# Queries and keys in two fp32r parts instead of three bf16 parts, two heads in 64-row tiles, and maxima and exponential units that alternate between the tiles

## The chip, the cores and the metric

One NeuronCore of a Trainium2 chip runs the whole program. The metric is device time in microseconds (us), from the first to the last instruction and what lies around them. The median of three runs of the kernel before is 1060.07 us (1059.28 to 1060.69).

## What is computed

The reference is a small transformer block on `x` of 4 x 1024 x 256 in float32: a mixture layer, a causal attention with 16 heads of 16, and the mixture layer again.

```python
def _L0_attn_ref(target, w_qkv, w_proj, b_proj, ln_gamma, ln_beta):
    qkv = target @ w_qkv                       # 256 -> 3 x 256; q, k, v: (4, 16 heads, 1024, 16)
    ...
    scores = einsum('bhqd,bhkd->bhqk', q, k) * (1.0 / np.sqrt(HD))      # HD = 16
    scores = scores * causal - (1.0 - causal) * NEG
    attn = softmax(scores, axis=-1)
    out = einsum('bhqk,bhkd->bhqd', attn, v)
    x = out @ w_proj + b_proj + target
    return (x - mu) * rsqrt(var + EPS) * ln_gamma + ln_beta

def _L0_ffn_ref(x, w_router, b_router, w_experts, b_experts):
    # router softmax over 8 experts, the best two chosen, their outputs added
    ...
x = x + 0.5 * ffn(layernorm(x))
x = x + attn(layernorm(x))
x = x + 0.5 * ffn(layernorm(x))
```

## The kernel before

**Stages.** The program has three stages that share the engines. The *front* (0 to about 340 us) runs the first mixture layer over eight chunks of 512 tokens (`NCH`), and for each finished chunk makes the values (`values`, L766) and the queries and keys (`queries_keys`, matmuls in `pair_product`, L346). The *attention* (about 340 to 823 us) runs over 16 groups (`NG`) of four heads of one batch element. The *back* (to the end) projects, normalises and runs the second mixture layer. Neighbouring stages overlap by a few steps: the front's last chunk already works on the maxima of group 0, and `lead` puts steps of the back between the blocks of the last two groups.

**Queries and keys.** A bank of 128 features x 512 tokens of float32 is split into three bf16 parts: ScalarE copies the first part out (`qk_hi`, L605), VectorE subtracts it (`qk_rests`, L992), ScalarE copies the second part (`qk_mid`, L609) and GpSimd subtracts that (`low_parts`, L469). SyncE stores the parts to `q_parts` and `k_parts` in HBM and `load` (L1256, L1258) brings them back for each group, into `qs` and `ks` with the 16 features of a head repeated in six pieces: 96 rows (`ROWS`), four heads side by side. The six pieces are the products of parts that are kept. Three more rows, 96 to 98, hold ones in `ks` and the negated maximum of each query, split in three bf16 parts, in `qs`.

**Attention, on each engine.** Each group needs two passes over the scores.
- *Maxima.* TensorE makes scores with queries on the partitions (`max_scores`, L1295, one of 38 `munits` per bank of 512 columns) and, for a block on the diagonal, adds the mask with one more matmul of 128 columns (L1298: `ident_b` times `masked_b`). VectorE reduces each bank to row maxima (`max_read`, L1322). After the last unit TensorE transposes the maxima (L1288), and VectorE splits them in three parts (L1307 to L1317), which SyncE places in the rows 96 to 98 of `qs` (L1347).
- *Exponentials.* TensorE makes the scores again with keys on the partitions and 99 rows, so that the maximum is subtracted (`exp_unit`, L1449, 38 units), ScalarE takes the exponential of each bank into `probs` (L1428), and GpSimd clears what lies above the diagonal (L1401).
- *Products.* For each of 12 blocks of keys, TensorE multiplies `probs` by the values (`products`, L1465) in float32, four heads at once in four tiles of 32 columns.

**Order.** It is written out by hand. In the slot of group g, TensorE issues an exponential unit of g, then one entry of a stream of maxima: the units from number 14 on of group g + 1, then three new ones of g + 2, the transpose for g + 1, and the rest of the first 14 of g + 2. The products stand a block or two behind their exponentials. Maxima have three banks (`ms`), exponentials three (`es`), outputs two (`os`). TensorE takes its instructions in order: a maximum unit waits until VectorE has read the bank three units back (`mread`), an exponential unit until ScalarE has read its bank (`expd`).

**In the last chunk of the front**, 16 maximum units of group 0 stand between the expert products (`takes_first`), 19 more between the steps behind it (`first_scores`, `FIRST`). The first of them waits for the constants of the mask, which GpSimd makes in `ready_group0`.

## Time and profile before

| | |
|---|---|
| median of 3 runs | 1060.07 us |
| the profiled execution, its own time | 1059.8 us |
| its span, first to last instruction | 1058.1 us |
| TensorE matmul busy | 1006.5 us, 95% |
| VectorE busy | 812.5 us, 77% |
| ScalarE busy | 533.6 us, 50% |
| GpSimd busy | 264.0 us, 25% |

A busy share is the union of an engine's instructions. The ends of matmuls are modelled, so matmuls that follow each other closely are seen best by the distance of their starts. The rows in the section below come from the page and from views of the trace: groups of instructions by shape, instructions in order of time, the waits, the chain of work that ended last, and busy time by stretches. In the chain a row is what held up the end at that time.

### The profile page before, as it was taken

Reading aid. Unit: us, or ns where it says so; the run is one execution under the profiler, and the core shown is the slowest. Engines: PE = TensorE matmul, PEld = TensorE weight load, DVE = VectorE, ACT = ScalarE, POOL = GpSimd, SP = SyncE. Lnnn points to the kernel's source line nnn. Section 1 sums busy time; section 2 is a strip of 40 time slices with the busy share of each in tenths; the row PEclk is TensorE's granted clock in tenths of the full one; section 3 lists DMA queues with packets and bytes.
Section 4 is the critical chain, followed back from the end, with each engine's and each line's share of the span. In section 5 each row is a group of like instructions: output and inputs, shape, how many; then the busy total and the mean of one; then the engine's idle time right before and its main releaser. Section 6 shows DMA issues by size and latency. Waiting matters only on the chain.

```text
span 1058.1 us, 20904 instructions
## 1 busy us (share of the span) xinstructions
PE 1006.5 (95%) x6050; PEld 606.7 (57%) x6050; DVE 812.5 (77%) x1795; ACT 533.6 (50%) x1042; POOL 264.0 (25%) x290
## 2 busy tenths in 40 slices
PE   6899999999987999999999999999987899999998
PEld 4677878787654343444444344433433677777776
DVE  5776767685766888888888888888857788888775
ACT  4225433543232677667777777777767423323210
POOL 1012211221323222221111111122322544344311
PEclk9999999999988899999999999999999999999999
DMA  7201101133144555544444555555130111101001
GB/s 231 65 1 61 60 0 59 60 81 42 57 89 91 62 72 73 66 60 62 59 62 62 62 71 71 72 72 73 35 103 9 51 61 61 50 28 42 20 21 40
DMA packets 55034, 63.99 MB, mean 60 GB/s; under 512 B 13776, under 2 KB 37312, under 8 KB 54976
## 3 DMA queue, kind: packets, MB, share of 16 engines
q1 hardware_dynamic: 54384, 62.47, 31.8%
q8 instruction: 29, 0.48, 0.2%
q10 hardware_dynamic: 592, 0.80, 0.2%
q14 instruction: 29, 0.24, 0.1%
HBM read 41.30 MB, written 21.23 MB: 59 GB/s over the span
## 4 chain that ended last, share of the span: by engine, by line
PE 86%; DVE 6%; ACT 3%; issue 2%; DMA 1%; POOL 1%; SPq 1%; DVEq 0%; POOLq 0%; ACTq 0%
PE bank L346 35%; PE bank L1465 14%; PE bank L1449 13%; PE bank L1295 13%; PE bank L766 3%; PE bank L1298 3%; PE bank L338 2%; PE bank L785 2%; ACT b_probs L1428 1%; DVE b_neg L1322 1%; DMA v_all<-L_ffn_w_experts 1%; DVE c_acc L982 1%; PE bank L735 1%; DVE a_st L301 0%; DVE a_acc L982 0%
## 5 line engine op out<-in xcount | busy, mean ns | idle before, releaser
L1322 DVE TENSOR_REDUCE b_neg<-bank 128x1 f32<-128x512 f32 (+3 forms) x608 | 366.0, 653 | 66.1 <-PE bank L1298 39.0
L1428 ACT ACTIVATE b_probs<-bank 128x512 f32<-128x512 f32 (+1 forms) x608 | 311.0, 577 | 132.6 <-PE bank L1449 130.8
L1295 PE MATMUL bank<-b_ks,b_qs 96*128 96x512 bf16 (+3 forms) x768 | 235.1, 336 | 16.1 <-DVE b_neg L1322 10.3
L1449 PE MATMUL bank<-b_qs,b_ks 99*128 99x512 bf16 (+3 forms) x768 | 222.2, 332 | 3.1 <-ACT b_probs L1428 2.7
L346 PE MATMUL bank<-we,a_xt 128*128 128x512 f32 x768 | 191.4, 402 | 1.9 <-DVE a_acc L982 1.9
L346 PE MATMUL bank<-we,c_xt 128*128 128x512 f32 x768 | 187.7, 399 | 1.9 <-DVE c_acc L982 1.9
L1401 POOL TENSOR_SCALAR_AFFINE_SELECT b_probs<-b_probs 128x512 f32<-128x512 f32 x128 | 83.0, 648 | 368.7 <-ACT b_probs L1428 368.6
L1465 PE MATMUL bank<-b_probs,b_vs 128*32 128x512 f32 (+3 forms) x1536 | 164.5, 500 | 1.7 <-POOL b_probs L1401 1.4
L346 PEld LDWEIGHTS bank<-we,a_xt 128*128 128x128 f32 x768 | 143.0, 191 | 31.7 <-DVE a_acc L982 1.6
L346 PEld LDWEIGHTS bank<-we,c_xt 128*128 128x128 f32 x768 | 141.8, 188 | 33.4 <-DVE c_acc L982 2.4
L1449 PEld LDWEIGHTS bank<-b_qs,b_ks 99*128 99x128 bf16 x768 | 65.8, 98 | 159.4 <-ACT b_probs L1428 119.0
L1295 PEld LDWEIGHTS bank<-b_ks,b_qs 96*128 96x128 bf16 x768 | 75.1, 99 | 65.7 <-DVE b_neg L1322 34.8
L1298 PE MATMUL bank<-b_masked_b,ident_b 128*128 128x128 bf16 x512 | 101.3, 223 | 0.0
L982 DVE SCALAR_TENSOR_TENSOR a_acc<-bank,a_mask,a_acc 128x256 f32<-128x256 f32 x192 | 81.5, 477 | 22.4 <-PE bank L346 21.4
L982 DVE SCALAR_TENSOR_TENSOR c_acc<-bank,c_mask,c_acc 128x256 f32<-128x256 f32 x192 | 81.5, 477 | 21.8 <-PE bank L346 21.3
L463 POOL TENSOR_TENSOR xs<-a_acc,a_acc 128x256 f32<-128x256 f32 (+1 forms) x32 | 24.8, 775 | 226.9 <-DVE a_acc L982 226.9
L1298 PEld LDWEIGHTS bank<-b_masked_b,ident_b 128*128 128x128 bf16 x512 | 51.1, 100 | 24.5 <-issue 0.3
L1465 PEld LDWEIGHTS bank<-b_probs,b_vs 128*32 128x32 f32 x1536 | 30.4, 108 | 55.8 <-issue 44.8
L463 POOL TENSOR_TENSOR xs<-c_acc,c_acc 128x256 f32<-128x256 f32 (+1 forms) x32 | 28.8, 900 | 99.9 <-DVE c_acc L982 99.9
L346 PE MATMUL bank<-a_xt2r,a_wqk 128*128 128x512 f32 x192 | 46.3, 396 | 0.8 <-DVE b_neg L1322 0.8
L469 POOL TENSOR_TENSOR a_part<-a_rest,a_part 128x512 bf16<-128x512 f32 x32 | 36.6, 1165 | 41.3 <-ACT a_part L609 41.3
L319 ACT ACTIVATE c_std<-c_mv,eps 128x4 f32<-128x4 f32 x16 | 4.6, 296 | 78.3 <-DVE c_mv L306 78.2
(134 smaller groups left out, 918.4 us busy)
## 6 DMA issues: line engine op xcount, KB each, us to landing
b_qs<-q_parts SPq DMA_DIRECT2D x96, 128.0 KB, 6.8
b_ks<-k_parts SPq DMA_DIRECT2D x96, 128.0 KB, 7.5
q_parts<-a_part SPq DMA_DIRECT2D x16, 384.0 KB, 2.7
k_parts<-a_part SPq DMA_DIRECT2D x16, 384.0 KB, 2.7
att_num<-b_oev SPq DMA_DIRECT2D x64, 64.0 KB, 7.6
c_num<-att_num SPq DMA_DIRECT2D x8, 512.0 KB
c_rec<-att_rec SPq DMA_DIRECT2D x16, 256.0 KB
out<-xs SPq DMA_DIRECT2D x8, 512.0 KB, 3.1
```

The costliest lines, as they stand in the source:

```text
L346: last = nc.tensor.matmul(out_, wa if x_moves else xa_, xa_ if x_moves else wa, start=(n == 0), stop=(n == len(steps) - 1))
L463: pool.tensor_tensor(s.xs[:, row(c, t), :].rearrange("p a d -> p (a d)"), acc[t % 2][0][:], acc[t % 2][1][:], ALU.add).then_inc(q.x_ready, 1)
L469: pool.tensor_tensor(part[j][:, 2, :], rest[j % 2][:], part[j][:, 1, :], ALU.subtract).then_inc(q.qk_lo, 1)
L766: last = nc.tensor.matmul(pt[pair][:, i * D:(i + 1) * D], xt2[:, h, t * P:(t + 1) * P], s.wv[:, h, :], start=(h == 0), stop=(h == DK - 1))
L982: dve.scalar_tensor_tensor(out=dst[:], in0=ring[n][:, i * D:(i + 1) * D], scalar=mask[par][:, t, 2 * n + i:2 * n + i + 1], in1=base, op0=A ...
L1295: last = nc.tensor.matmul(ms[bank][:, a * width:(a + 1) * width], qs[g.u][0:ROWS, c, i * P:(i + 1) * P], ks[g.u][0:ROWS, c, lo:lo + width] ...
L1298: last = nc.tensor.matmul(ms[bank][:, (a + 1) * width - P:(a + 1) * width], s.ident_b[:], masked_b[:], start=False, stop=True)
L1322: dve.tensor_reduce(dst, ms[bank][:, 0:len(heads) * width].rearrange("p (h w) -> p h w", w=width), AX.X, ALU.max, negate=True).then_inc(mr ...
L1401: pool.affine_select(out=part, in_=part, compare_op=ALU.is_ge, fill=0.0, base=0, pattern=[[0, GH], [1, P]], channel_multiplier=-1).then_in ...
L1428: act.activation(probs[b % 3][:, heads[0]:heads[0] + hp, 0:width], es[exp_bank(g, unit)][:, 0:hp * width].rearrange("p (h w) -> p h w", w= ...
L1449: last = nc.tensor.matmul(es[exp_bank(g, unit)][:, a * width:(a + 1) * width], ks[g.u][:, c, j * P:(j + 1) * P], qs[g.u][:, c, first_q:fir ...
L1465: last = nc.tensor.matmul(os_[half][SLOT * c:SLOT * (c + 1), start:CH], vs[g.u][:, j, c, :], probs[b % 3][:, c, 0:width], start=(j == 0), ...
```

## The change

- **Parts.** Queries and keys are split in two fp32r parts: ScalarE copies the first (`qk_hi`), VectorE subtracts (`qk_rests`) straight into the second. `qk_mid` on ScalarE and `low_parts` on GpSimd are gone. The parts in HBM are two of float32 instead of three of bf16.
- **Rows.** A head has three pieces of 16 rows, 48 rows (`ROWS`), and two rows for the maximum, 50 (`MROWS`). Two heads stand above each other: rows 0 to 49 and rows 64 to 113, and two pairs side by side. So a score matmul now names a tile of 64 rows x 128 columns, number t = 0 or 1.
- **Units.** Each unit of maxima or exponentials lies in one tile, and consecutive units of either kind change the tile. Group g still has 38 units of maxima; the exponentials have 40, since blocks of 128 columns hold two heads instead of four per unit. The stream of maxima keeps its order, but the transpose no longer takes a place when the stream is laid against the exponential units.
- **Mask.** It has 64 rows too and is added by two bf16 matmuls, of 128 and 64 columns, instead of one of 128. Its constants `pick` and `masked` take two memsets and four affine selects on GpSimd instead of one of each.
- **Maxima.** VectorE makes their two parts with two instructions instead of five; SyncE places them with four transfers instead of three.
- **Ones.** The rows of ones in `ks` come by two small transfers per buffer from `s.ones` instead of three memsets on GpSimd.

```diff
-ROWS = 6 * HD
-MROWS = ROWS + 3
-PARTS = ((0, 3), (3, 2), (5, 1))
+ROWS = 3 * HD
+MROWS = ROWS + 2
+PAIR = GH // 2
+HALF = P // 2
+Q_PARTS, K_PARTS = (0, 0, 1), (0, 1, 0)
...
-        def low_parts(m):
-            for j in range(4):
-                pool.wait_ge(q.qk_mid, at(4 * m + j + 1))
-                pool.tensor_tensor(part[j][:, 2, :], rest[j % 2][:], part[j][:, 1, :],
-                                   ALU.subtract).then_inc(q.qk_lo, 1)
...
-        def qk_mid(m, j):
-            act.wait_ge(q.qk_rest, at(4 * m + j + 1))
-            act.activation(part[j][:, 1, :], rest[j % 2][:], ACT.Copy).then_inc(q.qk_mid, 1)
...
                 dve.wait_ge(q.qk_hi, at(4 * m + j + 1))
-                dve.wait_ge(q.qk_lo, at(4 * m + j - 1))
-                dve.tensor_tensor(rest[j % 2][:], ring[j][:], part[j][:, 0, :], ALU.subtract).then_inc(q.qk_rest, 1)
+                dve.tensor_tensor(part[j][:, 1, :], ring[j][:], part[j][:, 0, :].bitcast(F32),
+                                  ALU.subtract).then_inc(q.qk_rest, 1)
...
+    pairs = [[(0, 0, P, p) for p in range(PAIR)] + [(CH // P, CH, P, p) for p in range(PAIR)]]
+    for i in range(1, KT):
+        for lo in range(0, (i + 1) * P, CH):
+            width = min(CH, (i + 1) * P - lo)
+            if (i, lo) == (CH // P, CH):
+                continue
+            if 2 * width <= CH:
+                pairs.append([(i, lo, width, p) for p in range(PAIR)])
+            else:
+                pairs += [[(i, lo, width, p)] for p in range(PAIR)]
+    return [(t, pieces) for pieces in pairs for t in range(2)]
...
-    return [[range(c, c + CH // width) for c in range(0, GH, CH // width)] for _, _, _, width in key_blocks()]
+    return [[(t, range(p, p + hp)) for p in range(0, PAIR, hp) for t in range(2)]
+            for hp in (min(PAIR, CH // width) for _, _, _, width in key_blocks())]
...
-        qs[u], ks[u] = sb(f"qs{u}", [MROWS, GH, SEQ], BF16), sb(f"ks{u}", [MROWS, GH, SEQ], BF16)
+        qs[u], ks[u] = sb(f"qs{u}", [P, PAIR, SEQ], F32R), sb(f"ks{u}", [P, PAIR, SEQ], F32R)
...
+            last = nc.tensor.matmul(ms[bank][:, begin:end], qs[g.u][rows, p, i * P:(i + 1) * P],
+                                    ks[g.u][rows, p, lo:lo + width], start=True, stop=not diagonal)
             if diagonal:
-                last = nc.tensor.matmul(ms[bank][:, (a + 1) * width - P:(a + 1) * width], s.ident_b[:],
-                                        masked_b[:], start=False, stop=True)
+                nc.tensor.matmul(ms[bank][:, end - P:end], pick[half, HALF:3 * HALF], masked[half, :],
+                                 start=False, stop=False)
+                last = nc.tensor.matmul(ms[bank][:, end - HALF:end], pick[half, 0:2 * HALF], masked[half, 0:HALF],
+                                        start=False, stop=True)
...
-            t, r, m = turned, turned_rest, mparts[g.u]
-            dve.tensor_copy(t[:], ms[bank][0:GH * KT, 0:P]).then_inc(mread, 1)
...
+            dve.tensor_copy(m[:, 0, :], turned).then_inc(mpart, 1)
+            dve.wait_ge(mpart, at(g.n + 1))
+            dve.tensor_tensor(m[:, 1, :], turned, m[:, 0, :].bitcast(F32), ALU.subtract).then_inc(mread, 1)
...
-                    while entries and entries[0][0] < unit0[b] + n:
+                    while entries and entries[0][0] - (entries[0][0] > turn_at) < unit0[b] + n:
```

**On TensorE, in the loop of the attention**, at the end of a block of 512 columns. `b_qs`, `b_ks` are queries and keys of a group, `b_probs` the exponentials, `b_vs` the values. Before:

```order
L1446 REGISTER_ALU
L1449 MATMUL bank<-b_qs_49,b_ks_50 128x512
L1285 REGISTER_ALU
L1295 MATMUL bank<-b_ks_74,b_qs_73 128x384
L1298 MATMUL bank<-b_masked_b,ident_b 128x128
L1465 MATMUL bank<-b_probs_56,b_vs_53 32x512 x4
```

After:

```order
L1470 REGISTER_ALU
L1475 MATMUL bank<-b_qs_49,b_ks_50 128x512
L1298 REGISTER_ALU
L1313 MATMUL bank<-b_ks_72,b_qs_71 128x384
L1316 MATMUL bank<-b_masked,b_pick 128x128
L1318 MATMUL bank<-b_masked,b_pick 128x64
L1492 MATMUL bank<-b_probs_56,b_vs_53 32x512 x4
```

The order of exponential unit, maximum unit and products is the same; a diagonal maximum unit has one matmul more. Along the stream the tiles of the score units run 0, 1, 1, 0, 0, 1, 1, 0: an exponential unit and the maximum unit behind it are in different tiles.

**On GpSimd, in the front before its last chunk**, where the mask's constants are made. `a_part` are the parts of queries and keys, `a_acc` the mixture's sums. Before:

```order
L463 TENSOR_TENSOR xs<-a_acc_108,a_acc_109 128x256
L469 TENSOR_TENSOR a_part_117<-a_rest_121,a_part_117 128x512
L469 TENSOR_TENSOR a_part_118<-a_rest_122,a_part_118 128x512
L469 TENSOR_TENSOR a_part_119<-a_rest_121,a_part_119 128x512
L469 TENSOR_TENSOR a_part_120<-a_rest_122,a_part_120 128x512
L1274 MEMSET b_masked_b 128x128
L1277 AFFINE_SELECT b_masked_b<-b_masked_b 128x128
L1267 MEMSET b_vs_72 128x32x16
```

After:

```order
L468 TENSOR_TENSOR xs<-a_acc_104,a_acc_105 128x256
L1275 MEMSET b_masked 128x128
L1276 MEMSET b_pick 128x192
L1280 AFFINE_SELECT b_pick<-b_pick 128x64
L1283 AFFINE_SELECT b_masked<-b_masked 128x64
L1287 AFFINE_SELECT b_pick<-b_pick 64x64
L1290 AFFINE_SELECT b_masked<-b_masked 64x64
L1271 MEMSET b_vs_70 128x32x16
```

The four subtractions ahead of the constants are gone and four instructions have come to them.

## Rows read from the trace of the kernel before

**Rows 1.** Stretches: length, busy us of PE, PEld, DVE, ACT, POOL, clock, DMA, GB/s.

```profile
343.20:353.30 10.10, 9.12 (x31) 3.54 (x32) 8.83 (x17) 3.86 (x7) 4.11 (x2) 0.50 0.68 88
370.30:744.80 374.50, 372.76 (x2929) 152.12 (x2927) 316.49 (x584) 265.94 (x521) 73.56 (x117) 1.00 0.52 66
773.50:824.00 50.50, 41.65 (x262) 16.93 (x263) 30.78 (x81) 35.72 (x69) 15.60 (x17) 0.94 0.14 39
```

**Rows 2.** The transposes of the maxima, one per group, between 365 and 750 us.

```profile
L1288 PEld LDWEIGHTS bank<-ident,b_neg x14: 97/97/97, 370.3 to 744.8; 128*32 128x32 f32 x14
```

**Rows 3.** Waits between 400 and 700 us: us in total, times, longest.

```profile
DVE b_neg L1322 <- PE bank L1298: 23.2, 51, 0.7
DVE b_neg L1322 <- PE bank L1295: 17.0, 31, 0.6
PEld bank L1295 <- DVE b_neg L1322: 11.7, 35, 0.7
```

**Rows 4.** TensorE in order of time in the loop: start us, length us, engine, line.

```profile
505.87 0.38 PE L1295 MATMUL bank<-b_ks,b_qs 96*128 96x512 bf16 x1
506.18 1.07 PE L1465 MATMUL bank<-b_probs,b_vs 128*32 128x512 f32 x8
507.18 0.39 PE L1449 MATMUL bank<-b_qs,b_ks 99*128 99x512 bf16 x1
507.41 0.38 PE L1295 MATMUL bank<-b_ks,b_qs 96*128 96x512 bf16 x1
507.63 0.38 PE L1449 MATMUL bank<-b_qs,b_ks 99*128 99x512 bf16 x1
...
508.50 0.22 PE L1298 MATMUL bank<-b_masked_b,ident_b 128*128 128x128 bf16 x1
508.56 0.38 PE L1449 MATMUL bank<-b_qs,b_ks 99*128 99x512 bf16 x1
```

**Rows 5.** TensorE in the front: fp32r matmuls, with a bf16 one between them.

```profile
22.17 0.23 PE L728 MATMUL bank<-ident_b,a_mask 128*128 128x128 bf16 x1
22.21 1.64 PE L346 MATMUL bank<-we,a_xt 128*128 128x512 f32 x6
...
152.24 4.12 PE L346 MATMUL bank<-a_xt2r,a_wqk 128*128 128x512 f32 x17
```

**Rows 6.** VectorE's split of the maxima between 400 and 700 us: busy us, mean ns.

```profile
L1317 DVE TENSOR_TENSOR b_mparts<-b_turned_rest,b_mparts 32x128 bf16<-32x128 f32 x11 | 4.7, 425 | 1.8 <-DVE b_mparts L1315 1.1
L1313 DVE TENSOR_TENSOR b_turned_rest<-b_turned,b_mparts 32x128 f32<-32x128 f32 x11 | 3.1, 280 | 0.4
L1307 DVE COPY b_turned<-bank 32x128 f32<-32x128 f32 x10 | 2.7, 269 | 0.0
L1311 DVE CAST b_mparts<-b_turned 32x128 bf16<-32x128 f32 x11 | 2.4, 215 | 1.1
```

**Rows 7.** The last chunk of the front, TensorE and GpSimd in order of time.

```profile
259.20 0.74 POOL L463 TENSOR_TENSOR xs<-a_acc,a_acc 128x256 f32<-128x256 f32 x1 [8.68 <-DVE a_acc L982]
267.49 0.29 POOL L1277 TENSOR_SCALAR_AFFINE_SELECT b_masked_b<-b_masked_b 128x128 bf16<-128x128 bf16 x1
...
267.84 0.23 PE L1295 MATMUL bank<-b_ks,b_qs 96*128 96x128 bf16 x1 [2.51 <-POOL b_masked_b L1277]
268.50 2.91 PE L346 MATMUL bank<-we,a_xt 128*128 128x512 f32 x6
```

**Rows 8.** The chain that ended last, at the seam from front to attention.

```profile
304.49 2.29 POOL a_part L469 x2
...
341.06 0.19 DVE b_turned L1307
...
343.65 0.48 DVE b_neg L1322
```

**Rows 9.** The weight loads: those of the attention (bf16) and of the front (f32).

```profile
L1295 PEld LDWEIGHTS bank<-b_ks,b_qs 96*128 96x128 bf16 x500 | 48.3, 98 | 26.4 <-DVE b_neg L1322 11.7
L346 PEld LDWEIGHTS bank<-a_xt2r,a_wqk 128*128 128x128 f32 x144 | 27.0, 188 | 6.5
```

174 lines of the change are left out of this document (96 added, 78 removed).

## The prediction

> **What bounds the kernel now.** I read the stretches first. In the steady part of the attention TensorE is busy 372.8 of 374.5 us, VectorE 316.5 and ScalarE 265.9, at the full clock [rows 1]. Fourteen transposes, one per group, start from 370.3 to 744.8 us [rows 2], so a group takes 374.5 / 13 = 28.8 us, of which VectorE works 24.3 and ScalarE 20.5. A busy TensorE can be a modelled one, so I looked at the distances of its starts. In the loop an exponential and a maximum matmul of 512 columns follow each other after 0.22 us (507.41 to 507.63), which is 512 columns at 2.4 GHz, its upper level; a mask costs 0.06 us (508.50 to 508.56), and the products of 512 columns hold it from 506.18 to 507.18, 1.0 us, with 0.1 us in front of them (505.87 + 0.22 to 506.18) [rows 4]. The waits agree: VectorE waits for TensorE 40.2 us in 300, TensorE's weight loads for VectorE 11.7 us [rows 3]. TensorE is the bound, VectorE 4.5 us per group behind.
>
> TensorE's group, from these rows: maxima and exponentials are each 18,432 columns, 36 matmuls of 512, so 72 x 0.216 = 15.5 us; 32 masks x 0.057 = 1.8; the 12 products are 6 of 512, 2 each of 384, 256 and 128 columns, which by the 1.0 us for 512 and about 0.2 us less for each 128 come to 9.4 us, and their 12 entries to 1.2. Sum 27.9 us; the other 0.9 us is waiting and the loop's own cost.
>
> **The change: score matmuls in the steady loop.** The trace of before shows no two row tiles, so this price is bounded from both sides. Below: two neighbours in different tiles run at the same time and the pair costs one. The nearest row is the products': eight matmul records in 1.07 us, in four column tiles [rows 4]; float32 takes four passes of 512 columns, 0.85 us, so four heads pass in the time of one. Above: they don't overlap, and each costs what an fp32r matmul costs alone. That is (4.12 - 0.39) / 16 = 0.233 us by the run of 17 [rows 5], 8% more than the 0.216 of bf16. So 36 pairs cost between 8.4 and 16.8 us against 15.5 now. I take the overlap: the products show that this array runs tiles side by side when its order lets it, and the order here puts neighbours in different tiles (0, 1, 1, 0, ...), so each unit finds the other tile free.
>
> The masks spoil part of it. A weight load of fp32r takes 188 ns, one of the bf16 scores 98 [rows 9]. Between fp32r matmuls a bf16 one of 128 columns costs more than its columns: six fp32r matmuls behind one end 22.21 + 1.64 = 23.85, when without it they would need 5 x 0.233 + 0.39 = 1.56; with the 0.04 in front that is 0.12 us for it [rows 5], which I put down to the next weights not being loaded under something so short. The unit behind a diagonal maximum is in the same tile, and the unit behind that can't start earlier. So a pair with a diagonal maximum of one head costs about 0.23 + 0.06 + 0.12 = 0.41 us (0.35 at 384 columns), not 0.23. Of the 38 units 16 have no diagonal: 16 x 0.233 = 3.7 us. Sixteen have one: 16 x 0.38 = 6.1. Four have two of 256 columns, about 0.6 each: 2.4. Two have four of 128, about 1.1 each: 2.2. The two added exponential units: 0.2. Sum 14.6 us against 17.3, a gain of 2.7. The products stay at 10.6. TensorE then needs 25.2 us.
>
> The Trainium skill ("TensorEngine Tiling (Array Packing)", Tiling Modes) says that different tiles can execute weight loads and matmuls in parallel; an estimate by that page's rule alone would have the masks hidden as well and pairs and masks at about 9.5 us, the case of the first rival below. "TensorE: Matmul & The Clock Gate" (Weight-path perf modes) speaks against the change: the fast weight load is not for fp32. The trace agrees with the second (188 against 98 ns [rows 9]); no run here shows the first for row tiles.
>
> **VectorE in the loop.** The reductions are as many and as wide. The split of the maxima loses three of five instructions: 269 + 215 + 280 + 215 (L1315, as L1311) + 425 = 1.40 us and some 0.3 of waits between them become one cast and one subtraction, 0.6 us [rows 6]. VectorE falls from 24.3 to 23.3 us per group. ScalarE has two units more; at its 20.5 us for 38 units and two copies that is at most 1.0 us, and it stays under 21.6. So TensorE at 25.2 stays the latest, VectorE now only 1.9 behind it. With the 0.9 of waiting kept, a group takes 26.1 us; some of that waiting was the loop's own, and the masks' hidden share is unknown, so I take 25.8: 3.0 us less per group. From the first group's second half to the last but one that is 14 groups: **-42 us**.
>
> **Transfers.** A group's queries and keys were 12 transfers of 16 rows x 4 heads x 1024 x 2 bytes and are 12 of 16 x 2 x 1024 x 4, the same bytes in pieces twice as long; they lie behind other work. The four placements of the maxima start some eight units before they are needed. Cost nothing; if a group took under 23 us, the cover for loads and placements would be thin. The parts of queries and keys are stored as 512 KB instead of 384, also under other work.
>
> **The front.** ScalarE loses 32 copies, GpSimd 32 subtractions, but the front's TensorE sends fp32r matmuls at their own distance of 0.233 us [rows 5], so in chunks 1 to 7 this is worth nothing. In the last chunk it is: the first maximum unit waited 2.51 us for the mask's constants, which stood behind `low_parts`; the next six expert matmuls then took 2.91 us instead of 1.64 at the half clock (1.2 GHz) [rows 7, 5]. GpSimd is now free at 259.9 us and needs, at 0.35 us for each of six instructions, until 262, before TensorE asks at 265.3. That is -2.5 - 1.3 = -3.8 us. Against it, each of the 16 maximum units there now changes the tiling from 128 rows to 64 and back. The nearest row is 0.1 us for a change before the products [rows 4]; two of them, and 0.1 us for the narrow mask and the fp32r weights: 16 x 0.3 = +4.8. Sum +1.
>
> **The seam.** The chain goes through ScalarE's second copy and GpSimd's two subtractions, 304.49 + 2.29, before VectorE goes on with the last chunk; now one VectorE subtraction, 0.7 us, ends about 304.6: -2.3. Later the split of the first maxima, from 341.06 to 343.65 [rows 8], shrinks to 0.7: -1.9. Then 10 us at half clock (343.20 to 353.30) [rows 1] hold some 8 us of score matmuls, worth -3.5 when paired. Sum -7.7. **The last two groups**: from 773.5 to 824 ScalarE is busy 35.7 of 50.5 us and the work of the back lies between [rows 1]; -1 for both.
>
> **The sum.** -42 + 1 - 7.7 - 1 = -49.7 us on the execution of 1059.8, which is within 0.3 us of the median: **1010 us**, faster by 4.7%.
>
> **The rivals.**
> - *VectorE becomes the bound.* The tiles hide the masks too: 36 x 0.233 = 8.4 us for pairs and, with the masks halved, 1 us more. TensorE falls to about 20 us and the group to VectorE's 23.3 plus a little, say 24.1: 14 x 4.7 = -66, with the rest -8: about 986 us. For it: four column tiles overlap without a visible cost. Against it: the order of instructions, since the unit behind a mask is in its tile. 0.18.
> - *The overlap is partial*: it sets in only where both units are ready at once, and TensorE's waits for VectorE (11.7 us in 300 now) and ScalarE undo half of it. A group at 27.6: -17, and about 1036 us. 0.14.
> - *The tiles don't overlap for fp32r* (slower). Then the score matmuls cost 16.8 instead of 15.5, the masks 32 x 0.12 = 3.8 instead of 1.8 at most, 32 x 0.09 = 2.9 at least: +2.4 to +3.3, with two weight loads that don't fit under narrow matmuls up to +4. 14 x 3.2 = +45, the front +5, the seam -4: about 1105 us (1090 to 1125). It decides from the point where a pair of 512 columns takes more than 0.43 us from start to start. For it: no row shows two row tiles at once; 0.16.
> - *The clock falls in the loop*, because TensorE now waits for VectorE: before, it fell to half where TensorE had waited for single steps of VectorE (343.20, after the split of the maxima), and at half clock the pairs cost 0.43 as before while the products double to 2 us. Also slower, some 1150 us, but a TensorE at the half clock is again fully busy and would be granted more. 0.03.
> - *The change does little, since VectorE and ScalarE waited only for the products*: within 0.2%. 0.02.
>
> **How the numbers follow.** The forecast has 0.47 and its own range 998 to 1023: the group between 25.0 and 26.6 us. From VectorE's case at 984 to the partial case at 1050 it holds about 8 in 10; the cases without overlap are left out above. Faster by over 0.2% (about what a measurement of this kernel tells from no change): 0.47 + 0.18 + 0.14 = 0.79; within: 0.02; slower: 0.19.
>
> **What would show it.** In the loop two score matmuls of different tiles start within a few hundredths of a us of each other, and pairs 0.23 us apart without a mask, 0.4 with one. The distance of the transposes is 25.8 us. TensorE no longer waits for GpSimd near 265 us, and the first exponential unit of group 0 starts near 341 instead of 348. VectorE is over 88% busy in the steady part. I am wrong if the starts of score matmuls of both tiles lie 0.23 us apart, or if TensorE's weight loads wait for VectorE by over 2 us per group: then VectorE is the bound.

## The result and the profile after

The changed kernel takes **1114.45 us** (median of four runs, 1110.68 to 1119.98). The kernel before took 1060.01 us beside it (four runs, 1059.28 to 1060.69): the ratio is 1.0519, interval 1.0494 to 1.0544. The change is slower by 5.2%; the forecast was 1010 us, and 1114 lies outside its range. The profiled execution has a span of 1108.9 us against 1058.1.

The page gives the first hint. Its line of 40 slices for TensorE's granted clock reads, for the changed kernel:

```profile
PEclk9999999999787699978996997899998899999999
```

The stretches of the attention follow, with the columns of [rows 1]: first group, four groups, a stretch of 23 us, two groups.

```profile
353.60:385.00 31.40, 30.03 (x174) 16.70 (x172) 22.26 (x39) 14.56 (x27) 3.10 (x5) 0.57 0.38 54
387.90:473.80 85.90, 84.52 (x772) 46.51 (x771) 71.27 (x125) 61.38 (x126) 16.90 (x27) 1.00 0.44 68
484.00:507.00 23.00, 21.95 (x119) 11.01 (x121) 11.78 (x19) 11.27 (x22) 3.10 (x5) 0.50 0.56 77
513.50:570.90 57.40, 56.44 (x515) 31.02 (x514) 47.65 (x84) 40.92 (x84) 11.27 (x18) 1.00 0.43 68
```

There are two kinds of stretches. Where the clock is whole, a group still takes 28.6 us: the transposes lie as follows (as [rows 2]; 387.9 to 473.8 in three groups, then one group alone).

```profile
L1301 PEld LDWEIGHTS bank<-ident,b_neg x4: 94/94/94, 387.9 to 473.8; 128*32 128x32 f32 x4
...
L1301 PEld LDWEIGHTS bank<-ident,b_neg x2: 94/94/94, 473.8 to 513.5; 128*32 128x32 f32 x2
```

85.9 / 3 = 28.63 us, against 28.8 before: 0.2 us was won where 3.0 were forecast. And three groups of the loop, one in three, took 39.7, 39.1 and 39.9 us instead. In each of them TensorE ran at 1.2 GHz, half its clock, for 20 to 24 us, though it was busy nearly all the time (21.95 of 23.00 us above).

The 50.8 us of the span divide so: the first transpose comes at 353.6 instead of 339.9 (+13.7); the first group lasts 34.3 instead of 30.4 (+3.9); from the second transpose to the last, 387.9 to 819.2, it is 431.3 instead of 403.2 (+28.1: three long groups at +11.0 each, the rest a little under before); what follows, +5.1.

**The tiles do overlap.** TensorE in order of time, columns as [rows 4]:

```profile
548.20 0.38 PE L1475 MATMUL bank<-b_qs,b_ks 50*128 50x256 f32 x1
548.20 0.50 PE L1313 MATMUL bank<-b_ks,b_qs 48*128 48x512 f32 x1
...
551.90 0.50 PE L1475 MATMUL bank<-b_qs,b_ks 50*128 50x512 f32 x1
551.90 0.73 PE L1313 MATMUL bank<-b_ks,b_qs 48*128 48x512 f32 x2
552.24 0.40 PE L1475 MATMUL bank<-b_qs,b_ks 50*128 50x512 f32 x1
```

Two units in different tiles start within 10 ns, where before they stood 0.22 us apart. But the pair does not cost the 0.233 us of one of them here: the next pair starts 0.34 us later (551.90 to 552.24). That is so in all 17 places of the loop at the whole clock where a pair of 512 columns follows another; each time the first one stands directly behind products. Before, the two units took 0.44 to 0.45 us. The low price does exist, as a kernel of experiment 2 shows (the changed one without masks), where one pair stands behind products and the next one doesn't:

```profile
506.17 0.50 PE L1470 MATMUL bank<-b_qs,b_ks 50*128 50x512 f32 x1
506.17 0.73 PE L1313 MATMUL bank<-b_ks,b_qs 48*128 48x512 f32 x2
506.51 0.62 PE L1470 MATMUL bank<-b_qs,b_ks 50*128 50x512 f32 x2
506.74 0.39 PE L1313 MATMUL bank<-b_ks,b_qs 48*128 48x512 f32 x1
```

From 506.17 to 506.51 it is 0.34 us again, then 0.23 to 506.74. So the overlap is there, and still the group kept its length.

**A stop at one place of the loop.** The waits of TensorE between 387 and 745 us (as [rows 3]) hold a line that the kernel before has not:

```profile
PE bank L1475 <- issue: 9.0, 3, 3.0
```

Three times TensorE issues nothing for 3 us and nothing in the record holds it. In order of time, the first of them:

```profile
481.57 0.51 PE L1475 MATMUL bank<-b_qs,b_ks 50*128 50x128 f32 x3
485.05 0.91 PE L1475 MATMUL bank<-b_qs,b_ks 50*128 50x512 f32 x2 [2.97 <-issue]
```

The others follow 578.8 and 675.2 us; the granted clock falls near them, at 483.5, 582.4 and 678.0. Such a line is easily read past: it says "issue", nobody's wait, and 9 us in 358 is little. It holds the key, as experiment 6 shows.

### The profile page after: what moved, and what is told of

Same layout as the page of the kernel before. It is cut to its first block, busy times and chain, and to the rows that moved or that the text cites. A ratio compares the mean times of both kernels' runs of the same rounds, so it can differ in the third digit from the quotient of the medians.

```text
span 1108.9 us, 21845 instructions
## 1 busy us (share of the span) xinstructions
PE 1049.0 (95%) x6562; PEld 692.1 (62%) x6562; DVE 804.0 (73%) x1747; ACT 519.3 (47%) x1042; POOL 216.8 (20%) x260
## 3 DMA queue, kind: packets, MB, share of 16 engines
q1 hardware_dynamic: 44284, 66.90, 28.1%
## 4 chain that ended last, share of the span: by engine, by line
PE 85%; DVE 6%; ACT 4%; issue 3%; DMA 1%; SPq 0%; POOL 0%; DVEq 0%; ACTq 0%; POOLq 0%
PE bank L350 35%; PE bank L1475 15%; PE bank L1492 15%; PE bank L1313 9%; PE bank L756 3%; ACT b_probs L1452 3%; PE bank L1316 2%; PE bank L775 2%; PE bank L342 2%; DVE b_neg L1345 1%; PE bank L1318 1%; DMA v_all<-L_ffn_w_experts 1%; DVE a_st L305 1%; DVE c_acc L972 1%; PE bank L725 1%
## 5 line engine op out<-in xcount | busy, mean ns | idle before, releaser
L1452 ACT ACTIVATE b_probs<-bank 128x512 f32<-128x512 f32 (+2 forms) x640 | 313.7, 557 | 166.3 <-PE bank L1475 161.8
L1313 PE MATMUL bank<-b_ks,b_qs 48*128 48x512 f32 (+3 forms) x768 | 283.6, 451 | 10.2 <-DVE b_neg L1345 7.1
L1475 PE MATMUL bank<-b_qs,b_ks 50*128 50x512 f32 (+3 forms) x768 | 264.3, 435 | 19.5 <-ACT b_probs L1452 9.3
L1475 PEld LDWEIGHTS bank<-b_qs,b_ks 50*128 50x128 f32 x768 | 127.1, 203 | 176.0 <-ACT b_probs L1452 134.5
L350 PE MATMUL bank<-we,a_xt 128*128 128x512 f32 x768 | 195.9, 409 | 1.9 <-DVE a_acc L972 1.9
L1492 PE MATMUL bank<-b_probs,b_vs 128*32 128x512 f32 (+3 forms) x1536 | 179.4, 542 | 1.2 <-POOL b_probs L1425 1.1
L350 PEld LDWEIGHTS bank<-we,a_xt 128*128 128x128 f32 x768 | 145.1, 194 | 33.5 <-issue 1.8
L1313 PEld LDWEIGHTS bank<-b_ks,b_qs 48*128 48x128 f32 x768 | 141.1, 204 | 33.5 <-DVE b_neg L1345 17.8
L1316 PE MATMUL bank<-b_masked,b_pick 64*128 64x128 bf16 x512 | 112.3, 239 | 0.0
L972 DVE SCALAR_TENSOR_TENSOR a_acc<-bank,a_mask,a_acc 128x256 f32<-128x256 f32 x192 | 81.5, 478 | 30.4 <-PE bank L350 29.6
L1318 PE MATMUL bank<-b_masked,b_pick 64*128 64x64 bf16 x512 | 93.0, 197 | 0.0
L1316 PEld LDWEIGHTS bank<-b_masked,b_pick 64*128 64x128 bf16 x512 | 49.0, 100 | 21.1 <-issue 9.9
L1318 PEld LDWEIGHTS bank<-b_masked,b_pick 64*128 64x128 bf16 x512 | 50.5, 103 | 0.0
```

The source lines that it names most:

```text
L350: last = nc.tensor.matmul(out_, wa if x_moves else xa_, xa_ if x_moves else wa, start=(n == 0), stop=(n == len(steps) - 1))
L972: dve.scalar_tensor_tensor(out=dst[:], in0=ring[n][:, i * D:(i + 1) * D], scalar=mask[par][:, t, 2 * n + i:2 * n + i + 1], in1=base, op0=A ...
L1313: last = nc.tensor.matmul(ms[bank][:, begin:end], qs[g.u][rows, p, i * P:(i + 1) * P], ks[g.u][rows, p, lo:lo + width], start=True, stop=n ...
L1316: nc.tensor.matmul(ms[bank][:, end - P:end], pick[half, HALF:3 * HALF], masked[half, :], start=False, stop=False)
L1318: last = nc.tensor.matmul(ms[bank][:, end - HALF:end], pick[half, 0:2 * HALF], masked[half, 0:HALF], start=False, stop=True)
L1452: act.activation(probs[b % 3][:, lane:lane + hp, 0:width], es[exp_bank(g, unit)][:, 0:hp * width].rearrange("p (h w) -> p h w", w=width), ...
```

## The experiments

Times are of one run unless it is said otherwise, each beside the kernel before on the same chip (1056.2 to 1060.3). One caution on small differences: the front's fall of the clock near 270 us is absent in some profiled runs of the same front, lasts 6.8 us in others and 17.1 in others again, and the first transpose comes at 346.8 to 353.6 us accordingly. So I compare groups of the loop, not totals, where less than 10 us matters.

**1. Do half-array tiles lower the clock?** The kernel before with 48 rows in every score matmul, which puts them in a tile of 64 rows. The order and the other engines' programs stay (the exponential units are cut to 48 rows by the same edit, not shown below).

```diff
-                                    ks[g.u][0:ROWS, c, lo:lo + width], start=True, stop=not diagonal)
+                                    ks[g.u][0:48, c, lo:lo + width], start=True, stop=not diagonal)
...
-                last = nc.tensor.matmul(ms[bank][:, (a + 1) * width - P:(a + 1) * width], s.ident_b[:],
-                                        masked_b[:], start=False, stop=True)
+                last = nc.tensor.matmul(ms[bank][:, (a + 1) * width - P:(a + 1) * width], s.ident_b[0:64, :],
+                                        masked_b[0:64, :], start=False, stop=True)
```

> The kernel before, but both score passes multiply 48 of the 96 and 99 rows, and the mask 64 of 128, so that every score matmul lies in one tile of 64 rows (it leaves out half of the products of the scores and the subtraction of the maximum). The matmuls are as many, as wide and, in one tile, one behind the other; only the rows of the array in use change. Theory A (the granted clock falls because the array's rows are used less): the clock falls to half for stretches of the loop as in the changed kernel, mean clock 0.95 or below, and the time is 1080 to 1120 us. Rival B (it falls because TensorE waits more): TensorE waits no more than before, so clock 0.98 and 1060 us within 5.

1423.7 us. Two more sizes, the same edit with 64 and with 80 rows (80 need the tile of 128):

> As the run with 48 rows in one tile, but with 64 rows of the scores (two of six parts and the subtraction of the maximum left out), which fill the tile. If the number of rows in use within the tile sets the granted clock, 64 rows raise it well over the 0.70 of 48 rows. If it is the half array that stands idle, it stays near 0.70 and the time near 1420 us, and rows of zeros in the changed kernel's tiles would bring nothing.

> The same with 80 rows, which no longer fit a tile of 64, so that each score matmul lies in the tile of 128 rows (one of six parts and the subtraction of the maximum left out). Theory A in the form 'a matmul in a half tile counts for less': clock 0.98 and 1060 us, as the kernel before. If rows in use count in proportion: clock between, 0.8 to 0.95, 1100 to 1250 us.

The time with 48 rows is far above even what Theory A expected. 64 rows: 1420.0 us. 80 rows: 1056.1 us. The same stretch of the three kernels, 48 rows first, then 64, then 80:

```profile
400.00:700.00 300.00, 300.00 (x1279) 99.00 (x1277) 150.36 (x252) 129.19 (x228) 32.62 (x52) 0.50 0.30 38
```

```profile
400.00:700.00 300.00, 300.00 (x1275) 98.71 (x1275) 149.56 (x251) 128.45 (x227) 32.53 (x52) 0.50 0.30 38
```

```profile
400.00:700.00 300.00, 298.13 (x2363) 121.38 (x2359) 255.71 (x472) 213.32 (x418) 60.26 (x97) 1.00 0.53 67
```

TensorE is busy 300.00 of 300 us and has half its clock for all of them; a group takes 53.1 us. In fact the clock fell at 343.8 and stayed low for 798.7 us. With the rows in a tile of 128 it is whole. So it isn't the rows in use in proportion, since 48 and 64 do the same, but the tile (a limit in rows between 64 and 80 would look alike): in these kernels a single tile of 64 rows, one at a time, doesn't bring the clock back, though TensorE is never idle. The Trainium skill ("TensorE: Matmul & The Clock Gate", Part 1) has the clock follow how busy TensorE has been; by the busy share alone, 300 of 300 us, this clock would be whole, and the measurement decides.

**2. The masks.** Both kernels without the mask matmuls (causality is left out of the maxima, so they are not the reference's). In the changed kernel:

```diff
-                                    ks[g.u][rows, p, lo:lo + width], start=True, stop=not diagonal)
-            if diagonal:
-                nc.tensor.matmul(ms[bank][:, end - P:end], pick[half, HALF:3 * HALF], masked[half, :],
-                                 start=False, stop=False)
-                last = nc.tensor.matmul(ms[bank][:, end - HALF:end], pick[half, 0:2 * HALF], masked[half, 0:HALF],
-                                        start=False, stop=True)
+                                    ks[g.u][rows, p, lo:lo + width], start=True, stop=True)
```

> The kernel before without the mask matmuls of the maxima (the maxima are then taken over all keys of a block). At the full clock TensorE loses 32 x 0.06 = 1.8 us per group: if TensorE is the bound the transposes are 26.9 us apart instead of 28.7 and the time falls by about 27 us. If waits for VectorE and ScalarE hold the loop, under 1 us per group.

> The changed kernel without the mask matmuls of the maxima. If the masks between fp32r units in their tile are what ate the gain of the overlap (theory M), a group at the full clock falls from 28.7 to 25 us or less, twice and more what the kernel before gains by the same edit. If the loop waits for ScalarE and VectorE anyway (rival W), it stays above 27.

Before without masks: 1034.8 us, a group 27.1 (-1.7). After without masks: 1044.1 us, a group 26.4 (-2.3), between the 25 of theory M and the 27 of rival W, so neither alone; and the three long groups are gone. The changed kernel's transposes and a stretch:

```profile
L1301 PEld LDWEIGHTS bank<-ident,b_neg x12: 93/94/94, 432.9 to 722.8; 128*32 128x32 f32 x12
```

```profile
459.30:670.40 211.10, 204.87 (x1546) 94.87 (x1545) 187.95 (x337) 161.73 (x336) 45.22 (x72) 1.00 0.51 72
```

I read this as "masks in one tile let the clock fall". That was wrong, as 6 shows: with the masks, 384 instructions of TensorE leave the body of the loop too.

**3. The masks' order.** The masks of a unit in two matmuls behind all its scores:

```diff
+        if wide[0]:
+            k = len(pieces)
+            ends = ms[bank][:, 0:k * width].rearrange("q (a w) -> q a w", w=width)
+            nc.tensor.matmul(ends[:, :, width - P:width], pick[half, HALF:3 * HALF],
+                             masked[half, :].unsqueeze(1).broadcast_to([HALF, k, P]), start=False, stop=False)
```

> The changed kernel with the masks of a unit behind all its score matmuls, in two matmuls per unit instead of two per piece (the same columns): in six units of a group 16 pieces have 12 of each mask's weight loads and 10 changes from bf16 back to fp32r weights less. Theory M/A together (masks hold one tile alone, which costs time at the full clock and makes the half array stand idle): at 0.1 us each a group at the full clock falls by 1.0 us from 28.7 to about 27.7 and the clock falls less often; 1060 to 1085 us. If the masks of the other units decide, 1095 or more.

1110.9 us; a group at the whole clock 27.9 us (-0.8), the long ones 43.7, 43.2, 40.4. Then the tiles of the maxima exchanged, so that an exponential unit and the maximum behind it share a tile:

```diff
-    return [(t, pieces) for pieces in pairs for t in range(2)]
+    return [(t, pieces) for pieces in pairs for t in (1, 0)]
```

> The changed kernel with the two tiles of the maxima exchanged (1, 0 instead of 0, 1), so that a maximum unit stands in the tile of the exponential unit ahead of it and runs beside the one behind it. Theory M: now the masks run beside the next exponential unit; a pair with a diagonal costs about 0.32 instead of 0.41 us, so a group at the full clock takes 27.3 instead of 28.7 us and the time falls by 15 to 25 us. Rival W: 28.7 as before, since the waits are elsewhere.

1186.4 us; a group 30.3 (+1.7), and one half-clock stretch of 122.9 us. So the order of tiles is worth something, but the opposite one gains nothing. A strictly alternating one, the maximum unit ahead of every second exponential unit, alone and with the masks in two:

```diff
-                    exp_unit(g, b, n)
+                    if (unit0[b] + n) % 2:
+                        exp_unit(g, b, n)
...
+                    if (unit0[b] + n) % 2 == 0:
+                        exp_unit(g, b, n)
```

> The changed kernel with the maximum unit ahead of every second exponential unit, so that the tiles of the score units alternate strictly (0, 1, 0, 1) and never stand in pairs (0, 1, 1, 0). If the masks' chain in one tile stops the other tile because the next unit in order is in the same one (the working of the prediction), a diagonal pair goes from 0.41 to 0.32 us: a group at the full clock falls by up to 1.4 us, to 27.3 or more. If waits for ScalarE and VectorE decide, it stays at 28.7 or grows, as exchanging the tiles did (30.3).

> Both edits together: the masks of a unit in two matmuls behind its scores, and strictly alternating tiles. If they add, 26.5 to 27.3 us per group at the full clock, and the half array idles less, so that the clock holds in the loop as in the run without masks: 1050 to 1070 us. If the clock falls again in three places: 1095 or more.

1123.9 and 1106.5 us; groups of 28.8 and 27.9, no better than the kernels without it. And the bank of the transposed maxima given free by a copy, before they are split:

```diff
+            dve.tensor_copy(turned[:], ms[bank][0:GH * KT, 0:P]).then_inc(mread, 1)
```

> The changed kernel, with the transposed maxima copied to SBUF first and their bank released after that, as the kernel before has it (three instructions instead of two). In the trace of the changed kernel the gap between products around the transpose is 2.81 us against 2.00 before. If the late release causes it, it falls by about 0.3 us (one instruction of 280 ns on VectorE), and a group from 28.7 to 28.4; if it is VectorE's own work that counts, the third instruction makes it 0.2 us longer. The clock as in the changed kernel: 1105 to 1120 us.

1112.4 us, groups of 28.7 to 29.2: nothing gained.

**4. The front.** The kernel before with the mask's constants ahead of GpSimd's subtractions, and the changed one with four maximum units instead of 16 in the front's last chunk:

```diff
+                if isinstance(c, int) and c == NCH - 2:
+                    a.ready_mask(pool)
```

```diff
-FIRST = (16, 23, 34, 35)
+FIRST = (4, 23, 34, 35)
```

> The kernel before with one edit: GpSimd makes the constants of the mask ahead of the four subtractions of the query and key parts instead of behind them. If the price put on this part of the change is right (a wait of 2.5 us and 1.3 us at the half clock), 1056.2 us, faster by 0.3 to 0.4%. If something else is late there, or the subtractions are missed later, 1059 to 1061.

> The changed kernel with 4 instead of 16 maximum units between the expert products of the front's last chunk; the other 12 come behind it. If these single units in a half tile let the clock fall there (17 us at half from 271.8), the fall goes or shortens and the first transpose comes earlier than 353.6 or no later than 356, though VectorE has 12 reductions of 0.65 us more behind the chunk (7.8 us). If the fall has another cause, it stays and the transpose is 5 to 8 us later.

The first: 1057.92 us (ten runs, 1056.27 to 1059.16) against 1058.89 (thirteen), ratio 0.9992, interval 0.9982 to 1.0001. Taking away the wait of 2.51 us [rows 7] is worth about 1 us, 2 at the most and perhaps nothing by the interval, and the trace says why. TensorE in order of time:

```profile
265.27 1.62 PE L346 MATMUL bank<-we,a_xt 128*128 128x512 f32 x6
269.09 0.28 PE L1299 MATMUL bank<-b_ks,b_qs 96*128 96x256 bf16 x1 [2.21 <-DVE b_neg L1326]
```

The next wait, for VectorE's reductions of the four banks that TensorE has filled in a burst, is 2.21 us long. The second: 1114.9 us. The fall near 271 us is gone and the first transpose comes at 342.7 instead of 353.6. The edit is not shown to be the cause of that: the first of the alternating variants of experiment 3, with all 16 units in place, has no fall there either, and its first transpose comes at 346.8. The seam (305.4, 23.9 us long) and the turns (up to 37.5 us) hold longer half-clock stretches in this run, and the total is the same.

**5. Who holds the group at the whole clock?** The reductions of VectorE over half the columns (the maxima are then of half the keys), in the changed kernel, the one before, and the changed one without masks:

```diff
+        scores = scores[:, :, :, 0:width // 2] if len(pieces) > PAIR else scores[:, :, 0:width // 2]
```

> The changed kernel, with VectorE reducing only the first half of each head's columns in a bank (the maxima leave out half of the keys). TensorE, ScalarE and the order are the same; VectorE's reductions take about 0.26 us less each, 10 us per group. If VectorE's pace holds the group at 28.7 us at the full clock (rival W for VectorE), it falls by 2 us or more. If the masks' chain on TensorE and the waits for ScalarE hold it, it falls by under 1 us. The clock may fall oftener or less often; the distances at the full clock count, not the time.

> The same edit to the kernel before. TensorE is the bound there: the group stays within 0.3 us of 28.7, and the time within 10 us of 1060.

> The changed kernel without masks (26.4 us per group, VectorE 89% busy) and with half reductions. TensorE's own sum there is 8.4 for the pairs and 10.6 for the products, 19 us; ScalarE's is about 20.5. If VectorE held it at 26.4, it falls to 23 or less. If it is the turn-taking of ScalarE and TensorE over three banks and the products, it stays above 25.

1116.6, 1049.4 and 1019.0 us; groups of 27.8 (-0.8), 28.4 (-0.4, a little more than expected with TensorE as the bound) and 25.5 (-0.9 against the one without masks). In the last, none of the engines is near its bound but TensorE by its modelled busy time, and ScalarE and TensorE wait for each other. Its stretch, then its waits:

```profile
400.00:700.00 300.00, 291.18 (x2288) 132.86 (x2290) 174.04 (x494) 238.15 (x497) 66.98 (x107) 1.00 0.52 76
```

```profile
PEld bank L1471 <- ACT b_probs L1448: 121.9, 225, 0.8
...
ACT b_probs L1448 <- PE bank L1471: 60.3, 117, 1.0
```

Half of VectorE's work gives 0.8 us, all the masks 2.3, both 3.2, and then 25.5 us are left, when the overlapped score matmuls and the products come to 19.2 (36 x 0.233 + 0.2 + 10.6, by the prediction's terms). Where the other 6 us lie these runs don't separate. Some are the dearer pairs behind products, by my estimate up to 12 x 0.107 = 1.3 us (0.34 less 0.233 for each of the 12 products). For the rest the waits above point to the turns of ScalarE and TensorE: TensorE waits for ScalarE to read a bank, and ScalarE then for the next units, with products between them. No run changed the number of banks or moved the products, so this is my reading and not shown.

**6. What makes the clock fall in the loop.** First, more work in whole-array tiles: the products of the first block of keys issued twice.

```diff
+            for lane in (range(GH) if j == 0 else ()):
+                c = head(*divmod(lane, PAIR))
+                nc.tensor.matmul(os_[half][SLOT * c:SLOT * (c + 1), start:CH], vs[g.u][:, j, c, :],
+                                 probs[b % 3][:, lane, 0:width], start=True, stop=True)
```

> The changed kernel with each group's two products on key block 0 (512 columns, float32, all rows and all four column tiles) issued twice, the first result overwritten: 2 us more of work on the whole array per group, 32 us in all. Theory A (the clock falls where the whole array is used too little): the clock holds or falls in fewer places, so that the time is at most 1115 us in spite of the added work. If the clock doesn't depend on it: 1140 us or more.

1129.1 us, a group 30.4 (+1.75); the half-clock stretches of the loop last 27.3, 10.2 and 10.2 us instead of 23.9, 20.5 and 23.9. The time lies between the two expectations. The added whole-array work doesn't prevent the falls; whether it shortens them is open, since one stretch is longer and two are shorter, and other variants differ from each other as much. All three start at the same place of the loop. That sent me back to the "issue" line. TensorE's program loops over three groups. The body was 1337 instructions and is 1535 (matmuls and weight loads counted apart; the trace has 1630 and 1828 records in a turn, mostly since it shows each float32 matmul and weight load of the products twice); the queue that brings instructions moves, between 400 and 740 us, before and after (packets, MB, share):

```profile
q8 instruction: 5, 0.08, 0.1%
```

```profile
q8 instruction: 31, 0.51, 0.7%
```

The loop turns three times. Before, no packet of this queue comes between 455 and 725 us: the body is repeated without being fetched. Now it comes again each time. After the change there are 7 packets between 487 and 577 us, within one turn, and one between 481 and 484 us, where the first stop is:

```profile
q8 instruction: 1, 0.02, 2.0%
```

Every variant above fits: bodies of 1145 and 1151 (without masks) and 1337 never stop, those of 1415 (masks in two matmuls), 1535 and 1583 (products twice) stop at every turn, 2.8 to 3.5 us each. Two kernels separate the cause. One writes the loop out on TensorE alone:

```diff
-        slots(pe, slot)
+        for n in range(NG):
+            slot(Group(0, 0) + n)
```

> The changed kernel with TensorE's loop over the groups written out (the 12 slots of the attention's loop stand one after the other, no branch; the other engines keep their loops). The records show that TensorE issues nothing for 3.3 us at 481.7, 578.8 and 675.2 us, each time at the turn of the loop, one of 3 groups, whose body on TensorE has grown from 1337 to 1535 instructions; q8, the queue of instructions, moves 31 packets between 400 and 740 us, 5 in the kernel before. 1.8 to 3.6 us after each of these stops the granted clock falls. Theory A (half-array tiles alone let the clock fall): the three stops go, -10 us, and the clock falls anyway somewhere in the loop; the slots of 39 us turn into at least two of 36, time about 1100. Theory T (the body no longer fits and is fetched again at the turn; that stop is what makes the clock fall, and the half-array tiles only keep it from coming back soon): no stop and no half-clock stretch between 385 and the last two groups, every slot at 28.7, 3 x 11 = 33 us less: about 1081. Theory F (code that is never repeated has to be fetched all the time and stops more often): stops of about 3 us in many slots, above 1115.

**1072.55 us**, 42 us faster than the changed kernel's median. The stretch over 12 groups and the transposes:

```profile
385.00:745.00 360.00, 353.65 (x3246) 192.49 (x3243) 300.66 (x529) 258.93 (x533) 73.01 (x117) 1.00 0.47 70
```

```profile
L1301 PEld LDWEIGHTS bank<-ident,b_neg x14: 94/94/94, 381.4 to 752.2; 128*32 128x32 f32 x14
```

No stop, no fall, 370.8 / 13 = 28.5 us for every group; 25 packets of instructions still come between 400 and 740 us, unnoticed, since they come in sequence. From the second to the last transpose it is 397.0 us (778.4 - 381.4) against 431.3 with the loop: 34.3 of the 38.1 us between the two spans. Against the kernel before it is 403.2, so at the whole clock the change does gain 6 us in the loop. It loses them and 13 more around it: the first transpose comes 7.2 us later, the first group takes 3.9 longer, and what follows the last transpose 7.8, all with longer half-clock stretches (27.3 us from 347.4, 13.7 from 815.0; before 10.2 and 3.4).

The other makes the body of the kernel *before* as long (1529), with its whole tiles, by splitting its mask in two:

```diff
+                nc.tensor.matmul(ms[bank][:, (a + 1) * width - P:(a + 1) * width - P // 2], s.ident_b[:],
+                                 masked_b[:, 0:P // 2], start=False, stop=False)
+                last = nc.tensor.matmul(ms[bank][:, (a + 1) * width - P // 2:(a + 1) * width], s.ident_b[:],
+                                        masked_b[:, P // 2:P], start=False, stop=True)
```

> The kernel before with its mask in two matmuls of 64 columns instead of one of 128, all 128 rows: TensorE's loop body has 1529 instructions instead of 1337, nearly as many as after the change, and the tiles stay whole. Theory T: three stops of about 3.3 us at the turns of the loop, and behind each the clock falls, but comes back within 3.4 to 10 us since the matmuls fill the array: three slots longer by 3.3 + 2 to 5 us, and q8 moves some 30 packets between 400 and 740 us. The 32 added matmuls of a group cost 0 to 0.04 us each, 0 to 1.3 us per group. Time 1060 + 3 x 5 to 8 + 0 to 18: 1075 to 1102. If the size of the body is not what stops TensorE: no stop, no half clock in the loop, 1060 to 1078. If whole tiles did not help the clock to come back: half-clock stretches of 20 us and more as after the change, above 1095.

1074.7 us, 15.6 more than before. Its stop and the waits of TensorE from 387 to 745 us, then the stretch behind the stop and the one after it:

```profile
467.95 0.60 PE L1451 MATMUL bank<-b_qs,b_ks 99*128 99x512 bf16 x2 [3.28 <-issue]
```

```profile
PE bank L1451 <- issue: 9.5, 3, 3.3
```

```profile
469.00:472.30 3.30, 3.30 (x31) 1.34 (x23) 1.57 (x3) 1.74 (x4) 0.04 (x1) 0.50 1.00 136
472.40:554.00 81.60, 81.17 (x723) 35.54 (x720) 68.33 (x129) 57.59 (x114) 15.62 (x25) 1.00 0.47 60
```

The same stop, and again the clock falls; but it is back after 3.4, 3.4 and 6.8 us, where the changed kernel needs 20 to 24. The three groups with a turn take 33.5, 33.5 and 34.3 us, where the same groups took 28.6 before; the others are within 0.1 us of before (so the 32 added matmuls cost nothing that shows). Together that is 15.6 us, 5.2 a turn, all that the time has grown by.

That gives each part its price. The length of the loop's body stops TensorE at three turns, about 3 us each, and with each stop the clock falls: about 5.2 us a turn in whole tiles. In the changed kernel the half clock lasts, and a turn costs 11. The Trainium skill ("Runtime: NRT & Kernel Launch", Instruction fetch mechanics) warns that a taken branch out of the window held breaks the sequential fetch. The trace agrees for bodies from 1415 instructions; that nothing shows at 1337 is the trace's, and where between the two it begins no run here shows. A combination of the loop written out and the masks in two was not run; by its parts it would be near 1062 us by my estimate (1072.55 - 13 x 0.8), no faster than before.

## Why the prediction was wrong, step by step

- **The score matmuls overlap** (rival "no overlap" at 1105): right, starts lie within 10 ns; the rival's time came near the measured one for another reason. **A pair of 512 columns costs 0.233 us**: wrong for a pair behind products, which costs 0.34 in all 17 places measured; the sum left the products at 10.6 and named no cost for the step from them to the pairs. The 0.23 shows only without masks, away from products.
- **TensorE needs 25.2 us, and with 0.9 of waiting kept the group takes 25.8**: wrong, 28.6. This is the step that failed in the loop at the whole clock: it carried -42 us, and it brought -0.2 to -0.3 a group. I added up TensorE's work and took the largest engine plus what it waited before. But the waiting needn't stay small when TensorE gets quicker: its loads and ScalarE can then wait for each other. Without the masks, the same sum says 20.1 us, and the chip 26.4; with half the reductions too, 25.5. TensorE's loads wait 121.9 us in 300 for ScalarE's banks there. Which of the waits sets this pace is not shown; that busy time plus the old waiting doesn't give it is.
- **The masks' chain in one tile, 6 us in a group**: as a cost on the path too large. Without masks the group is 2.3 us shorter (1.7 before), with the masks in two matmuls 0.8; the rest of the chain is not seen in the group's length. A mask is also cheaper than 0.06 + 0.12 us: its second matmul starts 0.07 us behind the first and the next fp32r matmul 0.03 us behind that, where nothing waits:

```profile
545.77 0.23 PE L1316 MATMUL bank<-b_masked,b_pick 64*128 64x128 bf16 x1
545.84 0.19 PE L1318 MATMUL bank<-b_masked,b_pick 64*128 64x64 bf16 x1
545.86 0.42 PE L1475 MATMUL bank<-b_qs,b_ks 50*128 50x384 f32 x1
```

- **VectorE 23.3 us a group**: 47.65 / 2 = 23.8, near. **ScalarE under 21.6**: 40.92 / 2 = 20.5, right. That neither was "the bound" didn't make TensorE the only one.
- **Transfers cost nothing**: right for data. For instructions I named no cost. I wrote that 32 masks become 64 and two units are added, and counted columns, never the loop's body, though the page of the kernel before has the queue of instructions (29 packets; after the change 57). The three turns cost 33 us.
- **The front, +1**: too small. The first transpose comes 13.7 us later in this run, and 6.9 to 8.2 us later in three variants with the same front (strict alternation, the copy before the split, the loop written out) where the half clock near 270 us lasts 0 to 6.8 us instead of 17.1. The wait for GpSimd went as foretold (the first unit starts at 265.56), but of its -3.8 us the experiment in the kernel before found about 1, since a wait for VectorE came next (2.21 us there, 1.21 here), which I had not looked for. The tiling changes, +4.8, were well sized: at the whole clock an expert step with a maximum unit but no mask takes 2.02 us (in the alternating variant, 298.75 to 300.77) against 1.72 before (294.74 to 296.46), 0.3 a unit. What the sum lacked is the half clock, which this run has from 271.8 to 288.9: TensorE is never idle, and six expert matmuls take 2.93 us instead of 1.64. The 7 to 8 us of the three variants I can only partly account for: behind 313 us they have one half-clock stretch of 17 to 21 us where the kernel before has two of 6.8. TensorE in order of time, then the stretch (columns as [rows 7] and [rows 1]):

```profile
269.50 0.32 PE L1313 MATMUL bank<-b_ks,b_qs 48*128 48x128 f32 x1 [1.21 <-DVE b_neg L1345]
...
273.67 2.93 PE L350 MATMUL bank<-we,a_xt 128*128 128x512 f32 x6
```

```profile
271.80:288.90 17.10, 17.10 (x48) 10.63 (x47) 6.68 (x15) 0.00 (x0) 0.72 (x1) 0.50 0.00 1
```

- **The seam, -7.7**: the split of the maxima shrank as said (the first exponential unit starts 6.6 us behind the first transpose instead of 8.4), and its gain went under the clock: 27.3 us at 1.2 GHz from 353.8 on, where before it was 10.2 from 343.1. The first group is 3.9 us longer. I had counted the pairs there as a gain *because* the clock was half; by experiment 1 the tiles are what can keep it half.
- **"The clock falls in the loop", 0.03, at about 1150**: the mechanism that decided. I dismissed it with "a TensorE at the half clock is again fully busy and would be granted more". The 48-row kernel is the counter-example, 300.00 of 300 us busy at 0.50. I also looked for the trigger in VectorE; in the loop it was code.
- **The signs**: besides the transposes, VectorE is 83% busy (47.65 of 57.40 us) and not over 88, and the first exponential unit starts at 360.2 us, not near 341. Neither of my two signs of being wrong showed: starts of different tiles are not 0.23 us apart, and TensorE's loads wait for VectorE 3.9 us in 358, 0.3 a group. I had no sign for ScalarE (94.8 us there) or for the clock.

What stays open: what holds a group at the whole clock beyond masks and reductions, why a pair behind products is dearer, why a stream in a single tile leaves the clock at half (only that it does is measured), why the stretches last mostly 20 to 41 us and in two variants 68 and 123, and where the last +5.1 us behind the last transpose come from beyond one longer half-clock stretch (13.7 us from 852.1).

## What to carry to other kernels

Count a loop's body in instructions of the engine before and after, and look at the queue of instructions and at the "issue" lines of the waits at the loop's turns; here each stop of 3 us at a turn also cost the whole clock. Row tiling halves the array that a lone matmul fills, and here the half clock after a stop lasted several times longer with it, so remove the stops first; and price a pair at each place where it stands, behind other tilings too. And a group's time isn't the largest sum of work plus the waits of before: where two engines wait for each other, take the work away in an experiment before believing what is left.

## What the runs showed of the hardware

- A matmul stream in single tiles of 64 rows (48 or 64 rows used) runs at 1.2 GHz for 798.7 us on end with TensorE busy all the time; 80 rows, in a tile of 128, at 2.4 GHz.
- A loop's body of 1337 instructions on TensorE turns without a visible stop; from 1415 on, TensorE stops for 2.8 to 3.5 us at each turn and the body comes again (5 against 31 packets in 340 us). Code in sequence, never repeated, comes without a stop.
- At or just behind such a stop the granted clock falls to half, in every kernel that had one: for 3.4 to 6.8 us in whole tiles, 10 to 123 in the tiles of 64 rows, mostly 20 to 41.
- Two fp32r matmuls of 512 columns in different row tiles start within 10 ns. The next pair follows after 0.34 us where the first stands directly behind products in tiles of 32 columns (17 of 17), after 0.23 to 0.24 us in 28 of the 34 other places, all in the changed kernels without masks. In the kernel before, splitting a mask of 128 columns into two of 64 cost nothing that shows (28.7 us a group either way).
